# Per-token attention's softmax done per half of the tokens, and its projections three steps earlier

## The reference, cut to what matters

```python
x = x + jnp.tanh(g_xattn[0]) * _L0_xattn_ref(_layernorm(x, axis=-1), ctx_1024, ...)   # causal attention, 16 heads
x = x + jnp.tanh(g_ffn[0]) * _L0_ffn_ref(_layernorm(x, axis=-1), ...)
```

```python
h = _rmsnorm(x, gamma1)
q = (h @ Wq + bq).reshape(b, t, H, HD)
kv = ((h @ Wdown + bdown) @ Wup + bup).reshape(b, t, H, 2 * HD)
k, v = jnp.split(kv, 2, axis=-1)
att = jnp.einsum('bthd,btgd->bthg', q, k) / np.sqrt(HD).astype(np.float32)
att = jax.nn.softmax(att, axis=-1)
out = jnp.einsum('bthg,btgd->bthd', att, v).reshape(b, t, D)
x = x + (out @ Wo + bo)
h2 = _rmsnorm(x, gamma2)
gate = jax.nn.softmax(h2 @ Wg + bg, axis=-1)
combined = jnp.einsum('btd,edf,bte->btf', h2, We, gate)
return x + combined
```

## Time and profile before

| | us |
|---|---|
| median of 3 runs | 2660.5 |
| lowest and highest run | 2658.87, 2661.01 |
| the profiled execution, its time | 2663.2 |
| the profiled execution, its span | 2661.4 |
| busy in the span: TensorE | 2325.5 (87%) |
| VectorE | 1487.3 (56%) |
| ScalarE | 1268.0 (48%) |
| GpSimd | 1019.5 (38%) |

### The profile page before, as it was taken

One profiled execution on the slowest core, in us unless ns is written; L12 is line 12 of the kernel. 1 busy time (PEld: TensorE's weight loads), 2 busy tenths in 40 slices (PEclk: granted clock), 3 DMA queues, 4 the chain that ended last, 5 costly groups with the idle time before them and its releaser, 6 DMA issues. The chain is left out here.

```text
span 2661.4 us, 48220 instructions
## 1 busy us (share of the span) xinstructions
PE 2325.5 (87%) x16128; PEld 1931.7 (73%) x16128; DVE 1487.3 (56%) x3906; ACT 1268.0 (48%) x3971; POOL 1019.5 (38%) x910
## 2 busy tenths in 40 slices
PE   5888989888888898888466999999999999999998
PEld 4667777777777777776354777877777887777777
DVE  3467667666766676767635445444444544444441
ACT  5655566555556555556023444433344443334441
POOL 1355554555554455555512333222233322223320
PEclk9989999999999999999667999999999999999999
DMA  4000000000000000000040000000000000000000
GB/s 145 14 6 17 13 16 4 16 16 16 16 12 4 16 16 16 16 4 9 4 161 1 13 17 16 16 16 16 4 12 16 16 16 16 16 4 12 16 9 9
DMA packets 25856, 51.66 MB, mean 19 GB/s; under 512 B 6272, under 2 KB 7040, under 8 KB 24640
## 3 DMA queue, kind: packets, MB, share of 16 engines
q1 hardware_dynamic: 25792, 50.84, 5.7%
HBM read 42.44 MB, written 8.39 MB: 19 GB/s over the span
## 5 line engine op out<-in xcount | busy, mean ns | idle before, releaser
L1191 POOL TENSOR_SCALAR l_probs<-l_probs,l_rinv 128x256 f32<-128x256 f32 x512 | 238.4, 480 | 590.0 <-DVE l_rinv L1406 589.4
L1302 ACT ACTIVATE l_probs<-l_score,l_negmax 128x256 f32<-128x256 f32 x512 | 238.4, 472 | 265.0 <-DVE l_negmax L1401 265.0
L364 POOL TENSOR_TENSOR l_prod<-l_att,l_kv 128x2048 f32<-128x2048 f32 x64 | 287.4, 4527 | 180.7 <-DVE l_att L637 180.7
L350 POOL TENSOR_TENSOR l_prod<-l_q,l_kv 128x2048 f32<-128x2048 f32 x64 | 290.3, 4547 | 155.9 <-DVE l_att L620 84.1
L1606 PE MATMUL l_ffn<-l_w,l_hid 128*128 128x256 f32 x1536 | 347.9, 382 | 1.0 <-ACT l_hid L1276 1.0
L1606 PEld LDWEIGHTS l_ffn<-l_w,l_hid 128*128 128x128 f32 x1536 | 287.6, 190 | 51.0 <-issue 14.3
L1413 DVE COPY l_probsT<-l_attn 128x512 f32<-128x512 f32 x256 | 175.5, 685 | 161.1 <-PE l_attn L1569 160.9
L710 DVE CUSTOM_DVE_ANT_0 l_probs<-l_score,l_mbias 128x256 f32<-128x256 f32 (+1 forms) x512 | 161.3, 353 | 147.5 <-PE l_score L906 97.6
L1401 DVE TENSOR_REDUCE l_negmax<-l_score 128x2 f32<-128x512 f32 x256 | 175.1, 684 | 65.4 <-PE l_score L1557 65.4
L643 DVE TENSOR_REDUCE l_h<-l_prod 128x128 f32<-128x2048 f32 x64 | 146.3, 2286 | 110.7 <-POOL l_prod L364 110.7
L439 ACT ACTIVATE l_probs<-l_probs,l_negmax 128x256 f32<-128x256 f32 x256 | 130.8, 511 | 107.7 <-DVE l_negmax L710 106.5
(11 more groups left out here) (271 smaller groups left out, 7527.2 us busy)
## 6 DMA issues: line engine op xcount, KB each, us to landing
l_ctxin<-in_ctx SPq DMA_DIRECT2D x32, 256.0 KB, 3.0
l_xin<-in_x SPq DMA_DIRECT2D x16, 256.0 KB, 2.7
l_x<-in_x SPq DMA_DIRECT2D x16, 256.0 KB, 2.6
x<-l_acc SPq DMA_DIRECT2D x16, 256.0 KB, 2.0
l_xin<-x SPq DMA_DIRECT2D x16, 256.0 KB, 3.3
l_x<-x SPq DMA_DIRECT2D x16, 256.0 KB, 2.6
out<-l_x SPq DMA_DIRECT2D x16, 256.0 KB, 2.0
l_hid<-in_w SPq DMA_DIRECT2D x2, 1536.0 KB, 8.6
```

Of the source, the lines that this page charges most:

```text
L350: nc.gpsimd.tensor_tensor(prod[:, u].rearrange("p (h g d) -> p h g d", h=half, g=H), q4[:, u * half:(u + 1) * half].unsqueeze(2).to_broadc ...
L364: nc.gpsimd.tensor_tensor(prod[:, u].rearrange("p (h d g) -> p h d g", h=half, d=HD), a4.unsqueeze(2).to_broadcast([P, half, HD, H]), v4.u ...
L1191: last = nc.gpsimd.tensor_scalar(probs[:, j % 4, t * S:(t + 1) * S], probs[:, j % 4, t * S:(t + 1) * S], rinv[:, j, t:t + 1], 1.0, ALU.mul ...
L1302: last = nc.scalar.activation(probs[:, s % 4, t * S:(t + 1) * S], ps[:, t * S:(t + 1) * S], ACT.Exp, bias=negmax[:, s, t:t + 1], accum_out ...
```

## The change

The projections of the per-token attention move: `hT` from step 2 to 1, `down` from 4 to 2, `q` from 3 to 2 and behind `down`, `up0` from 5 to 3, `up1` from 6 to 4; the order of PSUM uses in `side` follows. The four score reductions move from steps 7, 9, 11, 12 to 6, 7, 9, 10. Maximum, subtraction, exponential, sum, reciprocal and multiplication are done for each half of the tokens by itself: the maximum of a half at steps 7 and 10, the division at 8 and 11 (before 12 and 13 for both). The gathers move from 15, 16, 18, 19 to 11, 13, 14, 16. The first `weigh` of a half waits for that half's `att_ready`, and each of the first two `weigh` now also names the score reduction that frees its buffer.

```diff
--- before.py
+++ after.py
@@ -197,18 +197,18 @@
             attn_uses += [use for at, use in (own_at | ahead_at).items() if at == s]
         attn = Banks(nc, ctx, "l0_attn", attn_uses + ["out"], ahead=["xT", "k0", "k1", "k2", "v0", "v2"])
 
-        mix_at = {2: "hT", 3: "q", 4: "down", 5: "up0", 6: "up1"}
+        mix_at = {1: ("hT",), 2: ("down", "q"), 3: ("up0",), 4: ("up1",)}
         expert_at = {6: 0, 7: 1, 8: 2, 10: 3, 12: 4, 14: 5, 15: 6, 17: 7}
         add_at = {7: 0, 8: 1, 9: 2, 10: 3, 12: 4, 14: 5, 15: 6, 17: 7}
-        score_at = {7: 0, 9: 1, 11: 2, 12: 3}
-
-        gather_at = {15: 0, 16: 1, 18: 2, 19: 3}
+        score_at = {6: 0, 7: 1, 9: 2, 10: 3}
+        soften_at, divide_at = {7: 0, 10: 1}, {8: 0, 11: 1}
+        gather_at = {11: 0, 13: 1, 14: 2, 16: 3}
         score = Banks(nc, ctx, "l0_score", [f"s{j}" for j in range(H)] + ["idle0", "idle1"], 3)
         heads = Banks(nc, ctx, "l0_heads", [f"o{j}" for j in range(4)], 1)
-        mix_uses = ["hT", "q", "down", "up0", "up1", "idle"]
+        mix_uses = ["hT", "down", "q", "up0", "up1", "idle"]
         moe_uses = ["oT", "out", "h2T", "gate"] + [f"we{j}" for j in range(E)]
         side = SideBanks(nc, ctx, "l0_side", mix_uses, moe_uses,
-                         ["oT", "out", "hT", "q", "down", "h2T", "up0", "gate", "up1"] + [f"we{j}" for j in range(E)] + ["idle"])
+                         ["oT", "out", "hT", "down", "q", "up0", "up1", "h2T", "gate"] + [f"we{j}" for j in range(E)] + ["idle"])
 
         raw_in, split_hi, split_lo = [sem("raw_in0"), sem("raw_in1")], sem("split_hi"), sem("split_lo")
         mask_in, scored = sem("mask_in"), sem("scored")
@@ -355,8 +355,10 @@
                 def weigh(b, piece):
 
                     t, u, half = piece // 2, piece % 2, H // 2
+                    if u == 0:
+                        pool.wait_ge(att_ready, 2 * b + t + 1)
                     if piece < 2:
-                        pool.wait_ge(att_ready, b + 1)
+                        pool.wait_ge(scored, 4 * b + piece + 3)
                     else:
                         pool.wait_ge(gathered, 4 * b + piece - 1)
                     v4 = kv[:, t, D:2 * D].rearrange("p (d g) -> p d g", d=HD)
@@ -469,9 +471,9 @@
 
                 def before_exp(b, c, s):
 
-                    if b is not None and mix_at.get(s) == "hT":
+                    if b is not None and "hT" in mix_at.get(s, ()):
                         high(side, "hT", b, hT[0], hT_hi, gamma1)
-                    if b is not None and mix_at.get(s) == "down":
+                    if b is not None and "down" in mix_at.get(s, ()):
                         ps, full, _, turn = side.at("down", b)
                         act.wait_ge(full, turn)
                         nc.scalar.activation(dT[0][:], ps[0:LAT, 0:S], ACT.Identity, bias=bdown[:]).then_inc(dT_hi, 1)
@@ -490,13 +492,14 @@
                         for t in range(NT):
                             last = nc.scalar.activation(gate[:, t], gate[:, t], ACT.Copy, scale=gsum[:, t:t + 1])
                         last.then_inc(gate_ready, 1)
-                    if b is not None and s == 12:
-                        act.wait_ge(sub_ready, b + 1)
-                        nc.scalar.activation(att[:], att[:], ACT.Exp, scale=HD ** -0.5).then_inc(aexp_done, 1)
                     if a is not None and s in own_at:
                         project(own_at[s], a)
                     if nxt is not None and s in ahead_at:
                         project(ahead_at[s], nxt)
+                    if b is not None and s in soften_at:
+                        t = soften_at[s]
+                        act.wait_ge(sub_ready, 2 * b + t + 1)
+                        nc.scalar.activation(att[:, t], att[:, t], ACT.Exp, scale=HD ** -0.5).then_inc(aexp_done, 1)
 
                 def head_group(a, j):
 
@@ -620,22 +623,25 @@
                     V.tensor_reduce(att[:, t, u * P:(u + 1) * P], prod[:, u].rearrange("p (x d) -> p x d", d=HD),
                                     axis=AX.X, op=ALU.add).then_inc(scored, 1)
 
-                att3 = att[:].rearrange("p t (h g) -> p (t h) g", g=H)
-
-                def mix_softmax_max(b):
-                    dve.drain()
-                    V.tensor_reduce(amax[:], att3, axis=AX.X, op=ALU.max)
-                    dve.drain()
-                    V.tensor_tensor(att3, att3, amax[:].unsqueeze(2).to_broadcast([P, NT * H, H]), ALU.subtract).then_inc(sub_ready, 1)
-
-                def mix_softmax_divide(b):
-                    dve.wait_ge(aexp_done, b + 1)
-                    V.tensor_reduce(asum[:], att3, axis=AX.X, op=ALU.add)
-                    dve.drain()
-                    V.reciprocal(asum[:], asum[:])
-                    dve.drain()
-                    V.tensor_tensor(att3, att3, asum[:].unsqueeze(2).to_broadcast([P, NT * H, H]), ALU.mult).then_inc(att_ready, 1)
-                    dve.drain()
+                def heads_of(t):
+
+                    return att[:, t].rearrange("p (h g) -> p h g", g=H), slice(t * H, (t + 1) * H)
+
+                def mix_softmax_max(b, t):
+                    att3, of = heads_of(t)
+                    dve.drain()
+                    V.tensor_reduce(amax[:, of], att3, axis=AX.X, op=ALU.max)
+                    dve.drain()
+                    V.tensor_tensor(att3, att3, amax[:, of].unsqueeze(2).to_broadcast([P, H, H]), ALU.subtract).then_inc(sub_ready, 1)
+
+                def mix_softmax_divide(b, t):
+                    att3, of = heads_of(t)
+                    dve.wait_ge(aexp_done, 2 * b + t + 1)
+                    V.tensor_reduce(asum[:, of], att3, axis=AX.X, op=ALU.add)
+                    dve.drain()
+                    V.reciprocal(asum[:, of], asum[:, of])
+                    dve.drain()
+                    V.tensor_tensor(att3, att3, asum[:, of].unsqueeze(2).to_broadcast([P, H, H]), ALU.mult).then_inc(att_ready, 1)
 
                 def mix_gather(b, piece):
                     t, u = piece // 2, piece % 2
@@ -735,16 +741,16 @@
                             moe_squares(c)
                         if b is not None:
                             V.tensor_copy(x1res[:], x1[:]).then_inc(x1_copied, 1)
-                    if b is not None and s in mix_at:
-                        use = mix_at[s]
-                        if use == "hT":
-                            low(side, "hT", b, hT, hT_hi, gamma1)
-                        elif use == "q":
-                            mix_queries(b)
-                        elif use == "down":
-                            mix_down(b)
-                        else:
-                            mix_kv(b, int(use[2:]))
+                    if b is not None:
+                        for use in mix_at.get(s, ()):
+                            if use == "hT":
+                                low(side, "hT", b, hT, hT_hi, gamma1)
+                            elif use == "q":
+                                mix_queries(b)
+                            elif use == "down":
+                                mix_down(b)
+                            else:
+                                mix_kv(b, int(use[2:]))
                     if c is not None:
                         if s == 2:
                             moe_normalise(c)
@@ -766,11 +772,10 @@
                     if b is not None:
                         if s in score_at:
                             mix_scores(b, score_at[s] // 2, score_at[s] % 2)
-                            if score_at[s] == 3:
-                                mix_softmax_max(b)
-                        if s == 13:
-                            dve.drain()
-                            mix_softmax_divide(b)
+                        if s in soften_at:
+                            mix_softmax_max(b, soften_at[s])
+                        if s in divide_at:
+                            mix_softmax_divide(b, divide_at[s])
                         if s in gather_at:
                             mix_gather(b, gather_at[s])
 
@@ -955,18 +960,18 @@
 
                 def beside_head(b, c, s):
 
-                    if b is not None and s in mix_at:
-                        use = mix_at[s]
-                        if use == "hT":
-                            pe.wait_ge(h_ready, b + 1)
-                            transpose4(side, "hT", b, h)
-                        elif use == "q":
-                            side.emptied(pe, "hT", b)
-                            tokens(side, "q", b, hT, fq, D)
-                        elif use == "down":
-                            mix_down(b)
-                        else:
-                            mix_up(b, int(use[2:]))
+                    if b is not None:
+                        for use in mix_at.get(s, ()):
+                            if use == "hT":
+                                pe.wait_ge(h_ready, b + 1)
+                                transpose4(side, "hT", b, h)
+                            elif use == "q":
```

(6 more changed lines are left out.)

## The result

| | before | after |
|---|---|---|
| median, us | 2660.4 | 2862.2 |
| lowest and highest run, us | 2658.9, 2661.0 | 2859.1, 2866.3 |
| ratio, 95% interval | | 1.076, 1.0742 to 1.0779 |
| mean granted clock of TensorE | 0.956 | 0.917 |

The changed kernel is 202 us slower. The forecast was +26 us, and the range ended at 2712: the direction was right, the size was not.

A forecast was written before the change was run, and what follows sets the result against it. No engine is full, so waits decide; GpSimd and VectorE set a body's end, TensorE 1.5 us behind. A to D sum to +0.1 us, F adds 2.3: 14 x (0.1 + 2.3) - 7.5 (E) = +26 us, 2686 us; range 2641 to 2712.

The forecast's parts named there:

- C: VectorE from head 6's maximum to head 15's: 35.2 us in place of 33.6, +1.6 us a body.
- Rival 4: VectorE's softmax subtraction and multiplication slowed beside GpSimd's products: up to +1.6 us a body, 2677 us; chance 0.06.
- A: End of the body: earlier gathers remove TensorE's wait of 1.54 us for the last gather into `h`; -1.5 us a body.
- B: TensorE, steps 0 to 5: new waits for `h`, `hT_lo` and `h2T_lo`, with up1 ahead of head 6's scores; +2.5 us a body.
- F: TensorE's clock: one added fall a body from the new idle places in its early stretch; +2.3 us, bounds 0 and +4.6.
- D: Tail from head 15's maximum to the output product: a gather moves behind head 15's reciprocal; -2.5 us a body.
- E: Last element, where nothing hides the chain: GpSimd no longer waits 6.52 us for the softmax; -7.5 us, once.
- Rivals 1 to 3: No added clock fall, 2654 us (0.20); VectorE's stretch shorter than charged, 2636 (0.18); two added falls a body, 2719 (0.13).
- Rival 5: GpSimd still waits at the first `weigh`, some 3 us instead of 12.2, costing nothing; part of each case, no own chance.

The follow-up runs named there:

- clear: Changed kernel; both GpSimd products that started with a subtraction wait for it, divisions at steps 9 and 12, next element's normalisation at step 6: 2678.7 us.
- probes2: Kernel before with four added VectorE instructions at steps 5, 6, 7, 9 (reciprocal, strided copy, maximum, one-column copy): 2694.1 us, one run.
- proj: Kernel before with the moved projections alone, and their order of PSUM uses: 2694.0 us (1.0156).
- shift: Kernel before with the whole softmax, undivided, one step earlier, projections where they were: 2688.9 us (1.0112).

## Why the prediction was wrong

The 202 us are 183.5 that go with the holds (changed kernel against clear) and about 20 for all the rest together.

**C** is the term that failed, the stretch from head 6 to head 15: 35.2 us forecast, 46.84 measured. It counted each VectorE instruction at the length it has alone and charged nothing for standing beside a GpSimd product. Rival 4 named this and gave it a price: "the bounds are 0 and 0.4 us for each of the four", and "In the sum they are 0". The mechanism was named, the price was wrong by ten times: the two subtractions pay 3.8 us each, the two multiplications nothing in the full bodies (they fall into pauses), and the normalisation of the next input, which I had not seen, pays 2.1. Without holds C's 35.2 us are 35.48 in clear.

The 0.4 us came from `y`'s normalisation, 1.01 us beside GpSimd and 0.60 without. Read again, that row was a hold too: it starts at 729.54, and GpSimd's split of the context, 1.27 us long, ran from 728.87 to 730.14. Of that 0.6 us was left, so the row bounded nothing beside products of 4.5 us that have just started. And the trace of the kernel before has one row with the full price, which I overlooked: in the first body with per-token attention the same normalisation of the next input stands beside a product. GpSimd, then VectorE:

```profile
115.58 8.98 POOL L350 TENSOR_TENSOR l_prod<-l_q,l_kv 128x2048 f32<-128x2048 f32 x2 [3.32 <-DVE l_kv L616]
```

```profile
121.15 3.89 DVE L566 TENSOR_SCALAR l_xn<-l_xin,l_mvA,l_rstdA 128x256 f32<-128x256 f32 x2
```

The second product ends at 124.56; the first of the two instructions takes 3.56 us, where 410 ns is the median of the line's 32. A second reason stood against a high price: "the reductions beside products keep their 2.29 us". They do, but probes2 shows that a reduction is not of the held forms.

**A**, right: the output product starts at 819.50, the transposes of `oT` follow without a wait for `h`. **B**, right in the main: 1.87 us of waiting for `h` where 2.1 were forecast, 1.51 for `h2T_lo` where 1.7; the 0.4 us for `hT_lo` don't show. **F**: the clock falls in both places in the first stretch (0.50 from 744 to 747, 0.65 from 762 to 765), so two falls and not one; but B and F together are 4.2 us for 4.8 in this stretch. Alone (proj) they cost 2.5 us a body (35 over 14). **D**, right: 7.6 us from head 15's maximum to the output product, 7.2 forecast.

**E**: the last gather should come 7.5 us earlier. It does in clear (54.6 us after the last x1 store, 61.9 before), but in the changed kernel only by 1.4 (60.5): held instructions stand in that chain as well, the last element's two multiplications with 2.95 and 3.31 us.

With the holds away the forecast's sum comes near, 2686 us for clear's 2678.7, and this is in part luck: a full body is 1.4 us longer than before and not 2.4, the first body 5.4 us longer, and the end gains 9.8 us where E has 7.5. Rivals 1 to 3 moved the clock and VectorE's slack by tens of us; none could have given 200. Rival 5: GpSimd waited 7.15 us before the first product with v, not 3, because the reduction in front of it was late.

## What to carry to other kernels

Before an instruction of VectorE is moved beside one of GpSimd, look at its operands: with two SBUF inputs, or a copy or tensor_scalar from SBUF to SBUF, it can cost the rest of the GpSimd instruction, here ten times its own length. Bound such a price by the longest instruction of the other engine and not by the nearest slowdown in the trace. And ask each line that is a candidate for its longest instruction, not for its mean or for the one in the body that is being studied: the price stood once in the trace of the kernel before, in a body that I had not looked at. The remedies measured here: let GpSimd wait for the short instruction, put that one in a pause, or cut GpSimd's instruction.

## What the runs showed of the hardware

- The hold ends with the running GpSimd instruction, whatever the size of the held one: 4.50 us for 128x16, 4.78 for 128x256 beside products of 4.5 us, 2.10 when the products were cut in two. The product isn't slower for it (4.46 to 4.55 us).
- Held: tensor_tensor and scalar_tensor_tensor with two SBUF inputs, copy (strided too), tensor_scalar. Not held: reduction, reciprocal, a copy of one column, and a scalar_tensor_tensor with one of its two inputs in PSUM (L700 at 787.59 in the changed kernel, 0.87 us for two, beside the product from 787.00). The Trainium skill's page "SBUF — State Buffer" (Who interferes with whom) says that VectorE and GpSimd share a pair of ports as an exclusive lock, that the one issued second fully blocks, and that a reduction never contends. The rows here agree.
- The opposite order shows too, in small. In the kernel before, GpSimd's power for `y` (L316, 128x2) starts 0.17 us after VectorE's copy into `x1res` and takes 0.79 us; the median of the line is 0.69. At the start of the kernel the same line meets a subtraction of VectorE with two SBUF inputs and takes 1.16 us (VectorE, then GpSimd):

```profile
44.87 0.68 DVE L785 TENSOR_TENSOR l_fup_lo<-l_prod,l_fup_hi 64x512 fp32r<-64x512 f32 x1
```

```profile
44.96 1.16 POOL L316 TENSOR_TENSOR l_rstdA<-l_varA,l_neghalf 128x2 f32<-128x2 f32 x1
```

- Of the 11.4 us that clear wins in the middle of the body shown, 9.7 are holds. TensorE's slower clock behind them fits 1.3; some 0.4 were not traced. Why shift is slow was not settled either.
